# A fused patch-embedding, attention and mixture-of-experts kernel: an early piece of a table, stacked low-order products, block 0 gathered by matmuls

## The chip, the cores and the metric

The kernel runs on one core of one Trainium2 chip. The metric is the device time of one execution in microseconds (us); "before" is the median of three runs.

## What is computed

The reference joins three layers. Cut to what matters here (B = 8 batches, S = 164 tokens each, E = 192 columns, 12 heads, 16 experts):

```python
h = patches(x) @ proj_w.T + proj_b + pos_embed        # 36 image tokens a batch
h = concatenate([h, txt], axis=1)                     # + 128 text tokens = 164
# attention: xn = layernorm(layernorm(h)) * ln_w
avg_wte = mean(wte, axis=0)                           # wte is 50257 x 192
Q = xn[:, None] * W_qk[None, :, None, :]              # keys are the same as queries
attn = softmax(causal(Q @ Q.T / sqrt(192)))
out = (attn @ (xn - avg_wte)) / (position + 1)
h = h + out.reshape(B, S, 12 * 192) @ W_o.T
# switch layer: n = rmsnorm(layernorm(h)) * flnw, one expert of 16 a token,
# at most 64 tokens of a batch for one expert; the others get n itself
y = relu(n @ wi[e]) @ wo[e]
h = h + max_prob * where(kept, y, n)
```

## The kernel before

Everything stands in one program with a block of code for each engine; the order of the work is written out by hand, and the engines meet in semaphores.

**Attention.** Iteration b (0 to 6) finishes batch b and begins batch b+1; batch 7 (LAST) has its own tail. The 164 tokens are cut in 128 (part A) and 36 (part B). Each batch has five rounds of scores on TensorE (`score(b, r)`, r = 0 to 2 for A, 3 and 4 for B), for each a row maximum on VectorE (`row_max`), exponentials on ScalarE (`exps`), factors on VectorE (`row_factor`), and the scaling of P on GpSimd (`normalise`). P is transposed on TensorE (`p_transpose(b, q)`), q = 3 giving the first 128 keys of the B rows and q = 4 their last 36 keys. To multiply P and V exactly enough, each is split into a high and a low part (ScalarE copies the high part, `t_copy`, `values`; VectorE subtracts, `t_low`, `value_low`), and three products are added: high P by high V, high P by low V, low P by high V. `value(b, g)` does this into the banks bO (128 columns) and bE (the other 64 of a pair of heads); g = 3 is the round of the B rows, with 18 matmuls: three on the first 128 keys and three on the last 36, for each of one bO group and two bE groups. `project` multiplies by W_o into bank bJ.

**The table's mean.** The table has 28 chunks of 14 x 128 rows. Four chunks are loaded into four slots by SP; 18 more are added to them by accumulating DMAs that GpSimd issues (`add_wte`), each behind the one before it in the same slot; six are loaded in 12 half pieces by SP (`plain_loads`) into one buffer of two halves, and summed on VectorE (`plain_sum(b, k)`, two halves of columns for each of two half pieces). At the end VectorE adds the slots (`slot_add`) and reduces them (`table_total`, which ends with `wsum`); TensorE turns that into the mean (`wte_mean`), and `mean_projected` into a row that `mean_rows` subtracts from the token rows H. `h_transpose(n)` needs those rows.

**Switch layer.** After LAST's rows are finished, VectorE works out each token's expert and its place in a list of 112-row blocks (`routed`, `keep`, `place`; stage 0 has nine of the eleven slots of 128 rows, stage 1 the last two). GpSimd scatters the rows with 11 indirect DMAs to the DRAM tensor `dispatched`; SP waits until all are in (`scattered`), reads three blocks of rows back, and TensorE transposes the first (`x_transpose`). Each block then takes 12 matmuls into bO, 6 into bE, and an indirect DMA to the output. Rows that no expert keeps are worked out on VectorE and written by further indirect DMAs (`drow`, `dropI`). `stay_warm` is a run of matmuls whose result nobody reads.

## Time and profile before

| | |
|---|---|
| median of 3 runs | 367.31 us (365.68 to 370.08) |
| profiled execution, device time | 367.87 us |
| its span, first to last instruction | 366.0 us |
| busy: PE / VectorE / GpSimd / ScalarE | 334.5 / 228.0 / 167.7 / 126.2 us |
| mean granted TensorE clock | 0.967 of full speed |
| moved by DMA | 74.29 MB, mean 203 GB/s |

The profiled execution is 1.87 us longer than its span. Engines: PE is TensorE, DVE is VectorE, ACT is ScalarE, POOL is GpSimd, SP the engine that only issues DMAs; a q behind an engine's name is its instruction queue.

### The profile page before, as it was taken

To read this page: it belongs to the slowest core of one execution; us is meant where nothing else is said; L and a number is where in the kernel's file an instruction comes from. 1 tells how busy PE (TensorE), PEld (TensorE's weight loads), DVE (VectorE), ACT (ScalarE), POOL (GpSimd) and SP (SyncE) were. 2 spreads that over 40 slices of the span, in tenths; PEclk is the share of its full clock that TensorE was granted. 3 is DMA by queue.
4 is the path that set the end of the run, shared out by engine and by line. 5 is a ranking of instruction groups with operands and counts; after the bars stand their busy time and mean duration, and the time that the engine had idled before them with its cause. 6 is when DMAs were issued, how large, how long until landed. Compare 5 with 4: busy or idle time off the path is not lost.

```text
span 366.0 us, 6697 instructions
## 1 busy us (share of the span) xinstructions
PE 334.5 (91%) x2336; PEld 306.0 (84%) x2336; DVE 228.0 (62%) x557; ACT 126.2 (34%) x437; POOL 167.7 (46%) x180
## 2 busy tenths in 40 slices
PE   8499969899999999999998979999949999999992
PEld 3388859799899898997997969999815999999991
DVE  0669768789688787796888977657485222222221
ACT  2056543552545436534545024446610111111110
POOL 3173943755854846657548011250661134444321
PEclk9969989999999999999999978999998999999997
DMA  8899999289999995799997969400232699999940
GB/s 252 264 430 282 260 247 217 77 170 230 219 232 230 196 239 143 139 236 270 246 211 199 324 191 289 112 2 1 100 107 73 183 293 266 266 264 260 266 118 17
DMA packets 21096, 74.29 MB, mean 203 GB/s; under 512 B 3540, under 2 KB 9173, under 8 KB 20306
## 3 DMA queue, kind: packets, MB, share of 16 engines
q1 hardware_dynamic: 11362, 43.16, 38.5%
q0 software_dynamic: 6800, 27.82, 37.0%
q10 hardware_dynamic: 2912, 3.04, 3.0%
q8 instruction: 12, 0.20, 0.2%
q14 instruction: 10, 0.08, 0.1%
HBM read 66.12 MB, written 9.25 MB: 206 GB/s over the span
## 4 chain that ended last, share of the span: by engine, by line
PE 66%; DVE 13%; DMA 8%; ACT 5%; issue 5%; ACTq 1%; POOL 0%; POOLq 0%; DVEq 0%
PE bO L1224 18%; PE bS L1224 15%; PE bE L1224 14%; PE bJ L1224 12%; DMA wx<-in_wte 6%; ACT PB L563 2%; DMA hB<-in_txtB 2%; PE bT L1311 2%; DVE wx L856 1%; PE bT L1576 1%; DVE wbuf L856 1%; PE bT L1317 1%; PE bT L1270 1%; DVE oTA L823 1%; ACT pay L620 1%
## 5 line engine op out<-in xcount | busy, mean ns | idle before, releaser
L423 POOL TENSOR_TENSOR PA<-PA,rn 128x512 f32<-128x512 f32 x24 | 25.4, 1057 | 81.5 <-DVE rn L813 81.5
L401 POOL TENSOR_TENSOR AwA<-zT,w 96x512 f32<-96x512 f32 x45 | 50.1, 1192 | 17.4 <-ACT zT L540 17.4
L1224 PE MATMUL bJ<-wo_sb,oTA 128*128 128x192 f32 x288 | 52.7, 333 | 0.0
L558 ACT ACTIVATE PA<-bS,negmax 128x128 f32<-128x128 f32 x96 | 34.0, 367 | 51.3 <-DVE negmax L801 51.2
L1224 PEld LDWEIGHTS bS<-zT,AwA 96*128 96x128 f32 x384 | 47.3, 194 | 1.3 <-issue 0.2
L1224 PEld LDWEIGHTS bJ<-wo_sb,oTA 128*128 128x128 f32 x288 | 47.4, 194 | 0.0
L1224 PE MATMUL bS<-zT,AwA 96*128 96x128 f32 x384 | 47.1, 276 | 0.0
L1224 PE MATMUL bO<-PA,wx 96*128 96x112 f32 x384 | 45.4, 275 | 0.5 <-DVE PA L1197 0.5
L1224 PEld LDWEIGHTS bO<-PA,wx 96*128 96x128 f32 x384 | 44.9, 192 | 0.7 <-DVE PA L1197 0.7
L468 POOL DMA_INDIRECT out<-PA,yrow x16 | 15.1, 942 | 56.0 <-DVE PA L1213 56.0
L695 ACT ACTIVATE AwA<-bO 128x448 f32<-128x448 f32 x16 | 8.7, 544 | 78.5 <-PE bO L1224 52.9
L1224 PE MATMUL bE<-wx,AwA 128*112 128x192 f32 x192 | 33.9, 326 | 0.0
L838 DVE TENSOR_REDUCE wx<-wx 128x672 f32 (+1 forms) x24 | 31.7, 1326 | 2.2 <-DMA wx<-in_wte 2.2
L1224 PEld LDWEIGHTS bE<-wx,AwA 128*112 128x112 f32 x192 | 30.4, 177 | 0.0
L1206 DVE TENSOR_SCALAR AwA<-bO 128x224 f32<-128x224 f32 x16 | 6.3, 392 | 36.7 <-PE bO L1224 36.7
L576 ACT ACTIVATE oTA<-bO,lncol 128x512 f32<-128x512 f32 x24 | 16.6, 692 | 13.3 <-PE bO L1224 13.3
L801 DVE TENSOR_REDUCE negmax<-bS 128x4 f32<-128x512 f32 x24 | 16.4, 685 | 6.7 <-PE bS L1224 6.6
L1224 PE MATMUL bS<-zT,AwB 96*108 96x164 f32 x128 | 20.3, 302 | 0.0
L463 POOL DMA_INDIRECT dispatched<-pay,posI x11 | 12.4, 1125 | 16.3 <-ACT pay L620 12.1
L558 ACT ACTIVATION_READ_ACCUMULATOR PA<-bS,negmax 128x1 f32 x96 | 19.7, 205 | 0.0
L823 DVE TENSOR_SCALAR oTA<-bE,lncol 128x256 f32<-128x256 f32 x24 | 11.5, 480 | 12.8 <-PE bE L1224 12.8
L1224 PE MATMUL bO<-wo_sb,oTB 128*96 128x192 f32 x108 | 18.1, 327 | 1.0 <-DVE oTA L823 0.7
(252 smaller groups left out, 705.5 us busy)
## 6 DMA issues: line engine op xcount, KB each, us to landing
wbuf<-in_wte POOLq DMA_DIRECT2D x10, 1344.0 KB, 12.7
wx<-in_wte POOLq DMA_DIRECT2D x8, 1344.0 KB, 12.0
wx<-in_wi SPq DMA_DIRECT2D x16, 576.0 KB
wx<-in_wo SPq DMA_DIRECT2D x16, 576.0 KB
wx<-in_wte SPq DMA_DIRECT2D x12, 672.0 KB, 9.2
dispatched<-zeros SPq DMA_DIRECT2D x7, 675.5 KB, 9.0
wbuf<-in_wte SPq DMA_DIRECT2D x2, 1344.0 KB, 7.0
wx<-in_wte SPq DMA_DIRECT2D x2, 1344.0 KB, 17.6
```

Source lines behind the costliest of these rows:

```text
L401: nc.gpsimd.tensor_tensor(o, zT[:, k, ss].unsqueeze(1).to_broadcast(list(o.shape)), w2[:, k, hs].unsqueeze(2).to_broadcast(list(o.shape)), ...
L423: nc.gpsimd.tensor_tensor(t, t, q.unsqueeze(2).to_broadcast(list(t.shape)), ALU.mult).then_inc(p_ready, 1)
L463: nc.gpsimd.indirect_dma_start(out=xd[:, :], out_offset=bass.IndirectOffsetOnAxis(ap=posI[0:n, j:j + 1], axis=0), in_=pay[0:n, j, :], in_o ...
L468: nc.gpsimd.indirect_dma_start(out=out[:, :], out_offset=bass.IndirectOffsetOnAxis(ap=idx, axis=0), in_=rows, in_offset=None, bounds_check ...
L558: last = nc.scalar.activation(PA[:, h, :], bank[:, j * SA:(j + 1) * SA], ACT.Exp, bias=negmax[:, h:h + 1], accum_out=lsum[:, h:h + 1])
L563: last = nc.scalar.activation(PB[:, q, :], bank[0:HB * SB, j * SEQ:(j + 1) * SEQ], ACT.Exp, bias=negmax[0:HB * SB, 12 + q:13 + q], accum_o ...
L576: nc.scalar.activation(dst, src, ACT.Copy, scale=lncol[:, 0:1]).then_inc(o_used, 1)
L695: nc.scalar.activation(hT[:, 0:4, :], bO[0][:, 0:4 * T].rearrange("p (c n) -> p c n", c=4), ACT.Relu).then_inc(h0_ready, 1)
L801: nc.vector.tensor_reduce(negmax[:, 4 * r:4 * r + 4], bS[r % 2][:, :].rearrange("p (h s) -> p h s", h=4), X, ALU.max, negate=True).then_in ...
L823: nc.vector.tensor_scalar(dst, src, lncol[:, 1:2], None, ALU.mult).then_inc(e_used, 1)
L838: nc.vector.tensor_reduce(psums.rearrange("p (n e) -> p n e", e=EMB)[:, ds(2 * b + h, 1), q].rearrange("p n e -> p (n e)"), plain[h].rearr ...
L1224: return nc.tensor.matmul(o, l, r, start=start, stop=stop, skip_group_check=True)
```

## The change

Seven edits are made at once.

1. **Head.** The text rows are loaded in two parts, batches 0 and 1 first. The B rows (`hB`) are loaded three times, into partitions 0, 36 and 72. The w2 factors and the statistics of batches 0 and 1 come first on DVE; those of the other batches, the factors of batch 1 and the variances of batches 2 to 7 are moved.
2. **Plain piece.** SP issues the first plain piece ahead of the loads of slots 2 and 3; `plain_sum(0, 1)` stands behind `row_max(1, 1)`.
3. **Adds.** Iteration 0 issues one add instead of two, and iterations 1 to 5 three each (before 3, 3, 2, 3, 3).
4. **Stack.** The last 36 keys' high V, low V and high V lie in one tensor at partitions 0, 36 and 72 (the low one is written over), and P's in the same way, so that one matmul of 108 rows takes the place of three. GpSimd writes the last keys' P three times (`last_keys`). `value(b, 3)` has 12 matmuls.
5. **Table's sum.** In iteration 6, TensorE does `project(b, 0, 4)`, `p_transpose(b, 4)` and `score(LAST, 1)` ahead of `wte_mean`; on DVE `row_max(LAST, 0)` and `t_low(6, 3)` stand within `table_total`, and `mean_rows` stands behind `value_low(LAST)`.
6. **Block 0.** `select` writes for each slot a matrix of 112 columns that is one where a token's place is that column; TensorE multiplies the normalised rows by it (`dispatch`), and the result is block 0, transposed. Block 1's rows are the first that are read from DRAM.
7. **Dropped rows.** Their products are spread over the first two blocks, and the number of blocks is read behind block 0.

```diff
 # SP
             for s in range(2):
                 sp.dma_start(wchunk[s], wv[:, s, :]).then_inc(wte_first[s], 16)
             sp.dma_start(wo_sb[:, :, :], wo_attn).then_inc(wo_in, 16)
+            sp.wait_ge(tok_ready, 5)
+            plain_loads(sp, 0, 1)
             for s in range(2, WBUF):
                 sp.dma_start(wchunk[s], wv[:, s, :]).then_inc(wte_first[s], 16)
...
-            for q in range(XBUF - 1):
+            for q in (1, 0, 2):
                 rows(sp, q, q)
 # GpSimd
+            def last_keys():
+                for q0 in (0, 2):
+                    t, k = PB[:, q0:q0 + 2, SEQ:SEQ + SR].rearrange("p q (t s) -> p q t s", t=3), PB[:, q0:q0 + 2, SA:SEQ]
+                    nc.gpsimd.tensor_tensor(t, k.unsqueeze(2).to_broadcast(list(t.shape)),
+                                            rn[0:HB * SB, 12 + q0:14 + q0].unsqueeze(2).unsqueeze(3).to_broadcast(list(t.shape)),
+                                            ALU.mult).then_inc(pb_ready, 1)
...
                 weigh(b + 1, n, (0, 1), (1,))
                 for c in chunks[0:1]:
...
+                last_keys()
                 weigh(b + 1, n, (0, 1), (2,))
...
-                iteration(b, range(WBUF + 2 + 16 * b // 6, WBUF + 2 + 16 * (b + 1) // 6))
+                c = WBUF + 3 * b
+                iteration(b, range(c, c + 3) if b else (None, WBUF + 2))
 # DVE, head
+            dve.wait_ge(hb_in, 48)
+            text_stats(0, 2)
...
-            dve.wait_ge(vz_ready, 3)
+            dve.wait_ge(vz_ready, 2)
             z(0)
+            factors(1, 2, 2)
             dve.wait_ge(t_used, 1)
...
-            factors(1, 2, 2)
+            dve.wait_ge(hb2_in, 48)
+            text_stats(2, NBATCH)
             row_max(0, 0)
...
             row_factor(0, 2)
+            variances(2, NBATCH)
 # DVE, iteration(b)
-                plain_sum(b, 1)
+                else:
+                    plain_sum(b, 1)
                 t_low(b, 3)
                 row_factor(b + 1, 0)
                 t_low(b, 4)
                 row_max(b + 1, 1)
+                if is0(b):
+                    plain_sum(b, 1)
                 plain_sum(b, 2)
 # PE, value(b, 3)
                     else:
                         oo = o[:, 0:HEADS * SB].rearrange("p (h s) -> p h s", h=HEADS)
-                        mm(oo, vA[x][:, 0:E0], PTB0[y][:, :, :], i == 0, False)
-                        last = mm(oo, vB[x][:, 0:E0], PTB1[y][:, :, :], False, i == 2)
+                        last = mm(oo, vA[x][:, 0:E0], PTB0[y][:, :, :], i == 0, False)
+                if g == 3:
+                    last = mm(oo, vB[:, 0:E0], PTB1[:, :, :], False, True)
 # PE, iteration 6 and behind stage 1
                 p_transpose(b, 3)
-                if final:
-                    wte_mean()
                 project(b, 0, 4)
-                if final:
-                    mean_projected()
                 p_transpose(b, 4)
                 score(b + 1, 1)
                 if final:
-                    h_transpose(0)
+                    wte_mean()
                     pe.wait_ge(jb_used, 2)
                 value(b, 3)
                 if final:
-                    h_transpose(1)
+                    mean_projected()
                 project(b, 4, 10)
                 if final:
-                    h_transpose(2)
+                    h_transpose(0)
...
+            def dispatch(k0, k1):
+                for j in range(k0, k1):
+                    j0, _, sel = sels[j >= 6]
+                    for k in range(2):
+                        last = mm(bT[1][0:EC, k * T:(k + 1) * T], norm[:, j, k * EC:(k + 1) * EC], sel[:, j - j0, :],
+                                  j == 0 and k == 0, j == SLOTS - 1)
+                return last
...
+                if start:
+                    stay_warm(bJ, 6)
+                    x_transpose(1, 16)
 # DVE, behind place(B)
+            def select(B):
+                k0, k1 = STAGE[B]
+                link(nc.vector.tensor_tensor(part(posG, B), part(drop, B), part(posF, B), ALU.add))
+                for j0, j1, sel in sels:
+                    lo, hi = max(j0, k0), min(j1, k1)
+                    if lo < hi:
+                        bc = [128, hi - lo, T]
+                        nc.vector.tensor_tensor(sel[:, lo - j0:hi - j0, :], cst2[:, C_IO:C_IO + T].unsqueeze(1).to_broadcast(bc),
+                                                posG[:, lo:hi].unsqueeze(2).to_broadcast(bc), ALU.is_equal).then_inc(sel_ready, 1)
```

In iteration 6, DVE's order from the end of the table's sum (`wsum`) to the subtraction of the mean from the rows H (`H<-H,cN`), first before the change:

```order
L872 TENSOR_TENSOR wsum<-wsum,wtail 81x192
L877 TENSOR_TENSOR H<-bO,H 96x192
L801 TENSOR_REDUCE negmax<-bS 128x4
L958 SCALAR_TENSOR_TENSOR wr_sb<-bO,wr_sb 96x32
L962 TENSOR_SCALAR avg<-bO 128x2
L818 TENSOR_TENSOR PTB0L<-bT,PTB0H 128x432
L811 RECIPROCAL rinv<-lsum 128x4
L813 TENSOR_SCALAR rn<-rinv,cst 128x4
L966 TENSOR_SCALAR cN<-bO,cst 128x192
L967 COPY cS<-bO 128x192
L971 TENSOR_TENSOR H<-H,cN 128x768 x2
```

and with it, from `avg` on:

```order
L1004 TENSOR_SCALAR avg<-bO 128x2
L833 TENSOR_REDUCE negmax<-bS 128x4
L856 TENSOR_SCALAR oTB<-bE,lncol 128x6x36
L843 RECIPROCAL rinv<-lsum 128x4
L845 TENSOR_SCALAR rn<-rinv,cst 128x4
L861 TENSOR_TENSOR vAL<-zA,vAH 128x128
L863 TENSOR_TENSOR vAL<-zA,vAH 128x64
L861 TENSOR_TENSOR vB<-zB,vB 36x128
L863 TENSOR_TENSOR vB<-zB,vB 36x64
L1008 TENSOR_SCALAR cN<-bO,cst 128x192
L1009 COPY cS<-bO 128x192
L1013 TENSOR_TENSOR H<-H,cN 128x768 x2
```

The copy of value round 3 (`oTB`), a row factor and the four subtractions of `value_low` now stand between the mean and the rows from which it is subtracted.

PE's order in the same iteration, behind the last transposes of P's first 128 keys, before the change:

```order
L1315 MATMUL bT<-cst,PB 128x108 x4
L1224 MATMUL bO<-one,wsum 128x1
L1224 MATMUL bO<-one,wsum 64x1 x2
L1224 MATMUL bO<-wr_sb,one 96x16 x2
L1224 MATMUL bJ<-wo_sb,oTA 128x192 x4
L1224 MATMUL bO<-ws,avg 128x192 x2
L1317 MATMUL bT<-cst,PB 36x108 x4
```

and with it:

```order
L1386 MATMUL bT<-cst,PB 128x108 x4
L1293 MATMUL bJ<-wo_sb,oTA 128x192 x4
L1388 MATMUL bT<-cst,PB 108x108 x4
L1293 MATMUL bS<-maskA,idb 128x512
L1293 MATMUL bS<-zT,AwA 128x128 x8
L1293 MATMUL bO<-one,wsum 128x1
L1293 MATMUL bO<-one,wsum 64x1 x2
```

A projection, the last transposes and a round of scores moved ahead of the first matmul that needs `wsum`.

PE's order from the last ranks (`kp`) to block 0's first matmuls (`bO<-PA,wx`), before the change; 26 of the `bJ<-ones` rows are a run of `stay_warm`:

```order
L1224 MATMUL bT<-kp,ones 128x16
L1224 MATMUL bJ<-ones 128x512 x10
L1224 MATMUL bS<-cst,beC 1x27
L226 TENSOR_LOAD nbI
L226 ISA x2
L1224 MATMUL bJ<-ones 128x512 x26
L1576 MATMUL bT<-cst,AwA 96x112 x2
L1224 MATMUL bO<-PA,wx 128x112 x12
```

and with it:

```order
L1293 MATMUL bT<-kp,ones 128x16
L1293 MATMUL bT<-PA,pay 96x112 x6
L1293 MATMUL bT<-AwA,pay 96x112 x6
L1293 MATMUL bJ<-ones 128x512 x8
L1293 MATMUL bT<-AwA,pay 96x112 x4
L1293 MATMUL bS<-cst,beC 1x27
L1293 MATMUL bO<-PA,wx 128x112 x12
L1293 MATMUL bE<-wx,AwA 112x192 x6
L1293 MATMUL bJ<-ones 128x512 x6
L1662 MATMUL bT<-cst,AwA 96x112 x2
L234 TENSOR_LOAD nbI
```

Block 0 no longer stands behind the read of its rows (`bT<-cst,AwA`); that read is now block 1's.

## Rows read from the trace of the kernel before

**Rows 1.** The page: PE's granted clock in 40 equal slices of the span.

```profile
PEclk9969989999999999999999978999998999999997
```

**Rows 2.** Busy time by stretch: PE, PEld, DVE, ACT, POOL (instructions), PE's clock, DMA share, GB/s.

```profile
97.00:122.00 25.00, 24.45 (x177) 22.87 (x177) 19.86 (x37) 11.92 (x47) 16.03 (x17) 1.00 1.00 222
```

**Rows 3.** The chain of waits, in order of time: start us, us, what.

```profile
3.13 8.47 DMA hB<-in_txtB
...
27.30 20.47 DMA wx<-in_wte
...
78.71 1.18 PE bO L1224 x6
79.89 1.33 PE bE L1224 x12
...
103.55 1.17 PE bO L1224 x6
...
197.68 3.94 DVE wx L856 x2
...
226.97 1.95 PE bJ L1224 x12
229.36 2.00 PE bS L1224 x17
```

**Rows 4.** Instructions in order of time, the head: start us, us, what [idle before <- releaser].

```profile
14.81 0.35 DVE L750 TENSOR_TENSOR H<-bT,cS 36x192 f32<-36x192 f32 x1
...
18.96 0.45 PE L1270 MATMUL bT<-cst,zA 128*96 128x128 f32 x1 [4.81 <-DVE zB L795]
...
19.84 4.43 PE L1224 MATMUL bO<-wx 128*96 128x216 f32 x12
...
24.11 0.38 PE L1224 MATMUL bS<-maskA,idb 128*128 128x512 bf16 x1
```

**Rows 5.** The same view, iteration 0, DVE and PE.

```profile
43.01 2.63 DVE L773 TENSOR_SCALAR nmr<-mv 128x12 f32<-128x12 f32 x1
...
47.79 2.47 DVE L838 TENSOR_REDUCE wx<-wx 128x96 f32<-128x672 f32 x2 [1.56 <-DMA wx<-in_wte]
...
51.77 0.70 PE L1224 MATMUL bO<-PTB0H,vAH 128*128 128x432 f32 x1 [3.65 <-DVE PTB1L L818]
```

**Rows 6.** DMA queues between 36 and 42 us (q0: GpSimd's adds; q1: SP's).

```profile
q0 software_dynamic: 206, 1.02, 83.5%
q1 hardware_dynamic: 211, 0.43, 21.1%
```

**Rows 7.** Instructions in order of time: the last add, and SP's first zeros behind all adds.

```profile
184.30 1.20 POOL L412 DMA_DIRECT2D wbuf<-in_wte  x1
...
195.82 5.43 SPq L323 DMA_DIRECT2D dispatched<-zeros  x4
```

**Rows 8.** The same view, iteration 6.

```profile
214.86 0.69 PE L1224 MATMUL bO<-one,wsum 128*128 128x1 f32 x6 [2.67 <-DVE wsum L872]
...
221.08 1.83 DVE L971 TENSOR_TENSOR H<-H,cN 128x768 f32<-128x768 f32 x2
...
228.51 1.83 POOL L401 TENSOR_TENSOR AwB<-zT,w 96x432 f32<-96x432 f32 x2
```

**Rows 9.** The same view, from the last scatters to block 1.

```profile
272.58 2.54 DVE L1185 TENSOR_TENSOR H<-pay,flnb 128x1152 f32<-128x1152 f32 x4
273.56 2.37 POOL L463 DMA_INDIRECT dispatched<-pay,posI  x1 [0.30 <-issue]
...
277.60 1.27 SPq L242 DMA_DIRECT2D AwA<-dispatched  x3
280.68 0.36 PE L1576 MATMUL bT<-cst,AwA 112*96 112x112 f32 x2
...
281.51 2.93 PE L1224 MATMUL bO<-PA,wx 96*128 96x112 f32 x24 [0.48 <-DVE PA L1197]
...
286.43 2.83 PE L1224 MATMUL bO<-PA,wx 96*128 96x112 f32 x24
```

252 lines of the change are left out of this document (150 added, 102 removed).

## The prediction

> **What bounds the kernel now.** I read the granted clock by slices first, then the busy time by stretch, then the chain of waits, and last the single instructions wherever the chain leaves PE. PE's clock is full nearly everywhere, but lower in the slices from 18 us (a 6), from 46 us (an 8) and from 210 us (a 7 and an 8) [rows 1]; there the engine ran for some us at 1.2 instead of 2.4 GHz. In the body PE is the bound: 24.45 of 25 us busy at full clock [rows 2], and one batch follows the other in 103.55 - 78.71 = 24.84 us [rows 3]. The chain leaves PE in four places: at the head (the load of the B rows, 8.47 us, then the statistics), in iteration 0 (a plain piece that takes 20.47 us to land), at the table's sum in iteration 6, and at the scatter before block 0 [rows 3, 9]. Each low clock stands behind an idle time of PE there: 4.81 us, 3.65 us and 2.67 us [rows 4, 5, 8]. So an idle time costs itself and the slow matmuls after it. The change touches all four places and takes matmuls from the body. I name times of the trace of before throughout, as if nothing had shifted.
>
> **Head.** DVE begins the image rows at 14.81 [rows 4], because it first waits until 11.6 (3.13 + 8.47, [rows 3]) for all B rows and then works out eight batches of statistics. With a small first load it can begin when TensorE's image products and the first text rows are there. No row shows that moment apart; it lies between 10.8 and 12.5 by the order of the loads, and I take 11.2. From there to PE's transposes of z it is 18.96 - 14.81 = 4.15 us, less some 0.6 for the w2 steps that now come first: 14.8. PE is then hardly idle (its embedding ended at 18.96 - 4.81 = 14.15), so its clock should stay up, and the 4.43 us of the second embedding become 2.2 [rows 4]. The first scores, at 24.11, then begin at about 14.8 + 5.15 - 2.2 = 17.8: 6.3 us. Against it stand 432 KB more for the threefold B rows, for which SP's table loads wait: I put these 1 to 3 us later, so that GpSimd stands at its second add and scales the first P late. PE has gaps there that take most of that. Term: **-5.8** (bounds -4.0 and -6.5).
>
> **Iteration 0.** PE waits 3.65 us for the low parts before value round 3, since DVE stood 1.56 us for the plain piece and then summed two quarters of it, 2.47 us [rows 5]. The piece was behind slots 2 and 3 (2.75 MB) in SP's queue and beside GpSimd's adds. It now stands ahead of these slots. Beside the adds SP's queue moves 0.43 MB in 6 us (0.072 MB/us, [rows 6]), at worst 9.6 us for half a piece of 0.69 MB: issued at about 27 it lands before 38, while DVE wants it at 46. The Trainium skill, DMA: Bandwidth & Descriptors, "Queues, rings and completion order", says that each DMA engine goes round robin between the queues, a packet each. By that, SP's queue would get about half (0.12 MB/us of the same 0.24) and half a piece would take 5.7 us; the row's two queues moved 1.02 and 0.43 MB, so the trace does not bear out an equal share. Both end in time.
> What is late next is DVE itself. The 2.63 us of `nmr`, during which GpSimd weighed without pause [rows 5], goes from this place to where DVE is about to begin `t_low(0, 0)`; it may meet the scaling of P there and costs about 1.3 us before PE's first value round. One quarter sum, 1.24 us, is left ahead of `t_low(0, 3)`. I get value round 3 ready as PE ends `score(1, 1)`, so 3.65 us of idle time fall away and 1.3 are given back. Term: **-2.4** (bounds -0.5 and -3.7).
> From this round to the next one PE needs 78.47 - 51.77 = 26.7 us now (78.47 being where the round that the chain lists from 78.71 begins), against 24.84 in the body: slow clock and DVE's late rows [rows 3, 5]. With the idle time gone I expect the body's pace. The stack's saving belongs to it. So 26.7 - 24.0 = 2.7, less 0.4 because the add of iteration 0 must wait for slot 2, which now loads behind the piece: **-2.3** (bounds -0.5 and -2.9).
>
> **Stack.** Value round 3 takes 1.18 us for six matmuls into bO and 1.33 for twelve into bE [rows 3]. Two of six and four of twelve go: 0.39 + 0.44 = 0.84 us of PE. GpSimd pays for it: two more instructions of 216 columns; two of 432 took 1.83 us [rows 8], so 0.9 us, less 0.3 since the scaling has fewer columns. It ends about 1.2 us before PE's last transposes, and GpSimd is busy 16 of 25 us [rows 2]: nothing on the path; without that cover it would cost 0.6 us a batch. But PE and DVE are both nearly late here: DVE waited only some 0.65 us for that round, so its rows come at most 0.65 earlier. I take 0.68 a batch, for batches 1 to 5: **-3.4** (bounds -2.0 and -4.2). Batch 6 is in the next term. In LAST it gives nothing: behind it PE waits for a copy that DVE does after `place(0)`.
>
> **Adds.** Three a batch instead of 2.7. At 83.5% of 6 us for 1.02 MB [rows 6] an add of 1.376 MB costs 6.8 us of all engines, and at 21.1% for 0.43 MB a piece costs 4.1. Three adds and a piece: 24.4 us in a batch of 24.0 to 24.2, so the queue grows by 0.2 to 0.4 us a batch, 2 in all. The last add was issued at 184.30 and all had landed at 195.82; DVE needs it at 197.68 + 3.94 = 201.6 [rows 3, 7]. 5.8 us of cover less 2: **0**; beyond the cover each us costs a us.
>
> **Table's sum.** DVE's chain from 197.68 to `wsum` is unbroken; row maximum and `t_low` within it put its end at 216.3 instead of 214.8. PE fills the time with a projection (1.3 us; twelve records took 1.95), transposes (0.5) and scores (2.0, [rows 3]), and the 2.67 us of idle time and the slow clock behind it go [rows 8]. Value round 3 ends at 219.5 and the projection of six at 222.1. But then PE wants the mean subtracted. `mean_rows` now stands behind `value_low(LAST)`, which needs the exponentials of `score(LAST, 1)` and ScalarE's copies (222), and whose two-input subtractions wait behind GpSimd's AwB pair, 1.83 us [rows 8]: done at 224.2. Then 0.8 for the two copies and 0.9 for the first half of 1.83 us: 226.0. PE stands 3.9 us, more than the idle time it was spared, and comes back at half clock, which cost 2 to 3 us before. From there to the end of the projections I count 6.4 us at full clock plus 2.2: 234.7 against about 234.2 now, with the stack's 0.84 in it. Term: **+0.4** (bounds -2.0 and +2.0).
>
> **Block 0.** Before, SP reads the rows at 277.60, they are transposed at 280.68, block 0 begins at 281.51 and block 1 at 286.43 [rows 9]. Now block 0 needs only the places. These are known at 271.5; `select` has 224 columns in stage 1, and DVE's 2112 columns took 2.54 us [rows 9], so 0.3; the last four products (112 columns each, 24 records took 2.93 us) 0.9, the copy 0.4: block 0 begins near 273.6, 8 us early. Stage 0's `select`, 1.4 us, lies in DVE's wait for `project_b(2)`, and its 18 products take the place of `stay_warm`. But block 1 still needs the scatter: rows at 277.6, transposed at 280.7, started at 281.5, against 286.43. So only one block's time is won, 4.9, and a little more since the last scatter, 2.37 us beside DVE's products against about 1.0 for the others, now runs before them. I take 0.4 of it. Term: **-5.3** (bounds -3.5 and -6.2). The Trainium skill, SBUF — State Buffer, "Who interferes with whom", says that of a DVE instruction with two SBUF inputs and a GpSimd instruction that reads SBUF the second is fully blocked until the first ends. By that the 1.4 us would all go and the read come at 276.2, though PE is ready only at 280.0, so 5.6; the same rule is against the moved `nmr` and `value_low`, and the rows' 2.63 us agrees. The dropped rows' products lie in DVE's waits of the first two blocks: 0.
>
> **Sum.** -5.8 - 2.4 - 2.3 - 3.4 + 0.4 - 5.3 = -18.8. From the profiled 367.87 us: 349.1. The median of before lies 0.56 lower: **348.5 us**.
>
> **Rivals.** (1) The table's part goes well: DVE isn't held up in `value_low`, PE's idle time stays short and the clock up. For it: PE also went on at full clock behind small gaps. Against it: four instructions ahead of `mean_rows`. It gives 3 more: 345.5; 20%. (2) The adds land late: the body shortens by 0.7 a batch while the DMA engines were full already (share 1.00, [rows 2]). From 5.8 us of growth on, DVE waits at `slot_add`; at 10 it gives 353; 12%. (3) Block 0 does not give what it says: the added DVE and PE work delays the scatter, or block 1's rows land a block's time later: 353.8; 8%. (4) Slower than before: an accumulating add takes 8.3 us or more instead of 6.8 when three a batch stand beside the pieces. Then 15 adds need over 23 us more than DVE's cover and every gain is gone; at 9 us, 15 x 2.2 - 3.8 = 29 us of waiting give 378. Against it: 4.13 MB of adds went through in the 25 us of [rows 2], whose window holds three; 2%. The forecast has 55%; 3% I leave for more than (1).
>
> **How the numbers follow.** The range reaches over (1) and most of (2) and (3) and holds the bounds of head and table, which are the widest: 342.5 to 354.5. A measurement of this kernel can tell about 1% (3.7 us) from no change. Faster by more than that: all but (4) and a sliver, 97%; within 1%: 1%; slower: 2%.
>
> **What the profile after would show.** Right: the first scores near 18 us, PE's clock full until 40 us, no wait of DVE for the plain piece, 24.1 us a batch, an idle time of PE before the first rows of H are transposed, block 0's first matmul 8 us before block 1's rows are transposed. Wrong: half clock in the first 25 us, DVE waiting for an add at `slot_add`, or a second slow stretch behind iteration 0. The forecast fails most easily by the table's term and by the head, whose start no row shows.

## The result, and the profile after

The changed kernel takes 355.26 us, the median of 4 runs (351.50, 355.12, 355.41 and 355.53), against 367.15 us before (4 runs, 365.68 to 370.08). The ratio is 0.9643, with a 95% interval of 0.9555 to 0.9731. So the kernel is faster, as forecast, but by 11.9 us instead of 18.8, and the median lies 0.8 us above the end of the range. (The forecast was built on 367.31 us; 0.9643 of that is 354.2, just inside.) The profiled execution took 355.53 us (span 353.7) against 367.87. Executions that ran over 1.5% longer than the fastest of their kernel (four, two of them with the plain piece back and one of the last version) are left out where I compare.

First three lines of the page of the kernel after: the clock granted to PE, the DMA engines' share and their rate, in 40 slices of the span.

```profile
PEclk9998999999999999999999998999999999999997
DMA  7799999499999999999997979300338799999940
GB/s 242 157 420 274 297 350 251 74 244 244 194 240 249 207 226 224 246 233 286 214 207 234 283 206 273 89 2 1 114 118 240 230 285 237 231 222 247 239 117 11
```

The low clocks of [rows 1] from 18 and from 46 us are gone. One 8 stands from 27 us, where PE now waits for the scaling of P(0), and one from 212 us, behind the table's sum. (The 8 that [rows 1] has from 274 us, which the prediction doesn't list, fell on warming products, whose results nobody reads.) In the last quarter the DMA engines are full (six slices of 9), and in the last five of these they move 222 to 247 GB/s, against 260 to 266 in the kernel before. That line turns out to be the important one.

The chain of waits after, in order of time, answers to [rows 3]:

```profile
5.22 10.43 DMA hB<-in_txtB
16.11 9.69 DMA wbuf<-in_wte
26.10 1.23 POOL wbuf L422
...
46.60 2.58 DVE wx L871 x2
50.21 3.55 DVE vB L861
...
324.02 17.33 DMA wx<-in_wi
341.48 2.90 PE bO L1293 x24
```

At 26.10 GpSimd's second add is on it, at 50.21 DVE's low parts, neither of them before. The last two are new as well: the weights of the last block landed 17.33 us after their issue, and PE stood for them. To see where the time went, I followed the start of value round 3 of every batch (`vA[0]` against `PTB0`, 432 columns) and `xt_copy` of every block, since both stand in both kernels.

| us from the span's start | before | after | gained in all | forecast |
| --- | --- | --- | --- | --- |
| first scores (mask) | 24.11 | 17.93 | 6.2 | 6.3 |
| value round 3, batch 0 | 51.77 | 45.59 | 6.2 | 8.2 |
| value round 3, batch 1 | 78.47 | 71.19 | 7.3 | 10.5 |
| value round 3, batch 5 | 177.64 | 167.71 | 9.9 | 13.2 |
| value round 3, batch 7 | 252.76 | 241.88 | 10.9 | 13.5 |
| block 1, first matmul | 286.43 | 269.88 | 16.6 | 18.8 |
| last `xt_copy` | 356.99 | 344.73 | 12.3 | 18.8 |

(The forecast column adds up the prediction's terms in their order.) Two stretches missed: 3.2 us up to batch 1, nearly all of it behind the first scores, and 4.3 us in the blocks, where the forecast had nothing. The rest came out 1.0 us better.

**The head.** Instructions of the kernel after in order of time, to be held against [rows 4]:

```profile
11.39 0.35 DVE L778 TENSOR_TENSOR H<-bT,cS 36x192 f32<-36x192 f32 x1
...
15.06 0.31 PE L1339 MATMUL bT<-cst,zA 128*96 128x128 f32 x1 [1.45 <-DVE zB L827]
...
15.54 2.35 PE L1293 MATMUL bO<-wx 128*96 128x216 f32 x12
17.93 0.38 PE L1293 MATMUL bS<-maskA,idb 128*128 128x512 bf16 x1
...
26.10 1.23 POOL L422 DMA_DIRECT2D wbuf<-in_wte  x1 [2.90 <-DMA wbuf<-in_wte]
26.89 2.50 POOL L433 TENSOR_TENSOR PA<-PA,rn 128x512 f32<-128x512 f32 x2
...
26.40 3.15 DVE L861 TENSOR_TENSOR vAL<-zA,vAH 128x128 fp32r<-128x128 f32 x1
...
28.46 0.69 PE L1382 MATMUL bT<-cst,PA 128*128 128x128 f32 x4 [3.37 <-POOL PA L433]
```

DVE's image rows stand at 11.39 (estimated 11.2), z's transposes at 15.06 (14.8), the embedding takes 2.35 us (2.2) at full clock. Behind that two things are seen that the sum lacked. GpSimd waits 2.90 us for slot 1 before it can issue its second add, the scaling of P(0) stands behind it, and PE waits 3.37 us. And DVE's subtraction for the low parts, of two tiles in SBUF, takes 3.15 us where 0.28 is usual: it ends as GpSimd's run of work (26.10 to 29.39) ends.

**Block 0 to block 1**, PE of the kernel after, against [rows 9]:

```profile
262.98 2.93 PE L1293 MATMUL bO<-PA,wx 96*128 96x112 f32 x24 [0.34 <-DVE PA L1231]
...
269.05 0.36 PE L1662 MATMUL bT<-cst,AwA 112*96 112x112 f32 x2
269.88 2.93 PE L1293 MATMUL bO<-PA,wx 96*128 96x112 f32 x24 [0.48 <-DVE PA L1231]
```

Between batch 7's value round 3 and block 1, 28.0 us are left of 33.7: 5.7 us gained. Block 0's first matmul stands 6.1 us before block 1's rows are transposed. The prediction said 8, though its own times (273.6 and 280.7) give 7.1.

**The blocks.** Busy time by stretch in two stretches of 20 us that begin 18 to 20 us behind the start of block 1, before and after (PE, PEld, DVE, ACT, POOL, PE's clock, DMA share, GB/s). Before:

```profile
304.00:324.00 20.00, 20.00 (x159) 20.00 (x158) 5.07 (x18) 2.18 (x4) 8.32 (x9) 1.00 1.03 271
324.00:344.00 20.00, 20.00 (x158) 20.00 (x157) 4.94 (x16) 2.18 (x4) 7.57 (x8) 1.00 1.03 258
```

After:

```profile
289.00:309.00 20.00, 19.94 (x156) 19.58 (x155) 4.78 (x15) 2.17 (x4) 7.59 (x8) 1.00 1.03 241
309.00:329.00 20.00, 19.87 (x153) 19.19 (x151) 4.73 (x16) 2.17 (x4) 7.64 (x9) 1.00 1.03 233
```

The share is the same 1.03, so the engines are full in both; what they move fell from 258 to 271 GB/s to 233 to 241. Before, all 14 blocks behind block 1 took 4.81 us each. After, they do so until 297 us; the rest lose 4.2 us in all, 1.4, 1.5 and 0.5 of it on the last three.

The trace also shows how such a loss builds up. There are four places for weights, so a block's weights are asked for when the fourth block before it ends. In the change the `wi` load, half of a block's weights, took about 5 us from issue to landing for the first blocks served in this way and then ever longer, up to 17.3 us for the last. In the run with GpSimd's changed order (below), whose blocks lost nothing, it ended at 12.7 us, and there 14.1 us lie between this issue and the start of the block (323.2 and 337.3). So the blocks live on a stock of loaded weights that shrinks even at full engines, and the large losses come when it is used up. The trace of before doesn't hold these landings.

### The profile page after: what moved, and what is told of

Read it like the earlier page. It is cut to its first block, busy times and chain, and to the rows that moved or that the text cites. A ratio compares the mean times of both kernels' runs of the same rounds, so it can differ in the third digit from the quotient of the medians.

```text
span 353.7 us, 6667 instructions
## 1 busy us (share of the span) xinstructions
PE 322.4 (91%) x2304; PEld 298.4 (84%) x2304; DVE 225.1 (64%) x562; ACT 125.9 (36%) x437; POOL 171.3 (48%) x194
## 4 chain that ended last, share of the span: by engine, by line
PE 60%; DVE 14%; DMA 14%; ACT 5%; issue 4%; ACTq 1%; POOL 1%; POOLq 0%; SPq 0%; DVEq 0%
PE bS L1293 18%; PE bO L1293 13%; PE bJ L1293 11%; PE bE L1293 11%; DMA wx<-in_wi 5%; DMA hB<-in_txtB 3%; DMA AwA<-dispatched 3%; ACT PB L588 3%; DMA wbuf<-in_wte 3%; PE bT L1382 2%; DVE wx L889 1%; DVE vB L861 1%; DVE oTA L856 1%; DVE wbuf L889 1%; ACT PA L583 1%
## 5 line engine op out<-in xcount | busy, mean ns | idle before, releaser
L411 POOL TENSOR_TENSOR AwA<-zT,w 96x512 f32<-96x512 f32 x45 | 49.6, 1170 | 17.0 <-ACT zT L565 17.0
L1293 PE MATMUL bJ<-wo_sb,oTA 128*128 128x192 f32 x288 | 51.7, 328 | 0.0
L1293 PEld LDWEIGHTS bJ<-wo_sb,oTA 128*128 128x128 f32 x288 | 46.6, 191 | 0.0
L1293 PE MATMUL bS<-zT,AwB 96*108 96x164 f32 x128 | 21.4, 313 | 0.0
L601 ACT ACTIVATE oTA<-bO,lncol 128x512 f32<-128x512 f32 x24 | 16.6, 693 | 13.2 <-PE bO L1293 13.2
L1293 PEld LDWEIGHTS bS<-zT,AwB 96*108 96x108 f32 x128 | 19.5, 181 | 0.1
L1276 DVE CAST yrow<-AwA 112x1 int32<-112x1 f32 x16 | 2.4, 148 | 27.0 <-DMA out<-PA,yrow 27.0
```

The lines of the kernel that those rows point to most:

```text
L411: nc.gpsimd.tensor_tensor(o, zT[:, k, ss].unsqueeze(1).to_broadcast(list(o.shape)), w2[:, k, hs].unsqueeze(2).to_broadcast(list(o.shape)), ...
L601: nc.scalar.activation(dst, src, ACT.Copy, scale=lncol[:, 0:1]).then_inc(o_used, 1)
L1293: return nc.tensor.matmul(o, l, r, start=start, stop=stop, skip_group_check=True)
```

## The experiments

All are the changed kernel with the edit shown. They ran in three groups of four, each on one chip with its own runs of the kernel before (medians 367.80, 368.18 and 367.58 us). Only the first group holds the change itself, so the later ones are compared with it across chips. I call the time that the blocks behind block 1 take beyond 4.81 us each **the blocks' loss**, in the profiled execution.

**The change again, unaltered.**

> The changed kernel unaltered, as the measure for the other three and to see whether its profile repeats. In the first profile the blocks run at 4.81 us each up to 297 us and then lose 4.2 us to rows and weights that land late (three of them, 1.4 + 1.5 + 0.5 us, behind 320 us), while the DMA engines move 237 GB/s against 269 before. Theory A: this is what the chip's memory gave in that execution; then this profile may show none of it and about 351.5 us, as one of the four runs did. Theory B: it belongs to the changed kernel; then the blocks lose 3 to 5 us again and the time is 355 to 356.

354.71 us (354.23 to 355.98); ratio 0.9641 (0.9595 to 0.9688). The blocks' loss is 4.2 us again, at 246 and 253 GB/s in the same two stretches. Theory B, as far as two profiles can say. In front of the blocks the repeat isn't the same: value round 3 comes at 46.16 in batch 0, 72.70 in batch 1 and 242.34 in batch 7.

**Block 0 started as before.**

```diff
-            select(0)
-            select(1)
-            dispatch(...)                  # all 22 products
+            stay_warm(bJ, 26)
+            x_transpose(0, 16)
...
-            for q in (1, 0, 2):
+            for q in (0, 1, 2):
```

> The changed kernel with block 0 started as before: no select, no products that pick its rows, its rows loaded behind the scatter and transposed, the dropped rows computed ahead of the blocks. Theory A (the late loss is of the memory, not of this part): the blocks start 5 to 6 us later (block 1 at about 275.5 instead of 269.9) and the whole is 5 to 6 us slower than the changed kernel, if both have or both lack the late loss. Theory B (the early start causes the late loss): the blocks keep 4.81 us to the end, and the whole is only 1 to 2 us slower than the changed kernel, about 357.

The products of the dropped rows go back ahead of the blocks as well. 361.78 us (360.67 to 362.83), 7.1 above the unaltered change. PE in order of time:

```profile
268.47 0.40 PE L1649 MATMUL bT<-cst,AwA 112*96 112x112 f32 x2 [2.25 <-DMA AwA<-dispatched]
269.35 5.12 PE L1286 MATMUL bO<-PA,wx 96*128 96x112 f32 x24 [0.48 <-DVE PA L1229]
...
277.55 2.83 PE L1286 MATMUL bO<-PA,wx 96*128 96x112 f32 x24
```

From batch 7's value round 3 (240.84) to block 1's first matmul are 36.7 us against 28.0 in the change and 33.7 before. 3.1 of the 8.7 are not the part's worth: the warming products end 2.25 us before the rows are there, and block 0's first matmuls then run at 1.2 GHz (5.12 us against 2.93, and 3.08 against 2.17 for the second set; granted clock 0.56 from 269 to 275 us). The rest is 5.6, theory A's size. The blocks' loss is still 1.8 us with the old start. So the loss is not made by block 0's early start alone; theory B falls, the more so as six runs below keep the early start and lose nothing.

**GpSimd scales before its second add.**

```diff
             add_wte(WBUF)
+            normalise(0, (0,))
             add_wte(WBUF + 1)
-            normalise(0, range(3))
+            normalise(0, (1, 2))
```

> The changed kernel with one edit at the head: GpSimd scales the first quarter of P(0) before it issues the second add, which now waits 2.9 us for its slot. Theory: that wait holds PE 3.4 us before the first transposes of P (28.46 to 31.10), and with it gone PE is 2 to 3.4 us earlier at value(0,3); the whole is 2 to 3 us shorter. Rival: DVE's rows of PT or the second add, issued later, become the bound at once, and the time moves by less than 1 us.

351.77 us (350.22 to 353.57), 2.9 below the unaltered change, just what the theory said, and yet it is not the reason. PE's wait for P falls only from 3.4 to 2.2 us, value round 3 of batch 0 stands at 45.17, and DVE copies block 1's transposed rows at 269.40, 0.04 earlier than in the first profile and 0.52 earlier than in the second. The profile's gain lies in the blocks: their loss is 0.0, at 253 and 252 GB/s. The median alone would have confirmed a wrong theory. The rival is right on the head: other waits come at once. Value round 3 of batch 1 stands at 72.18, 1.0 later than in the change. One of these waits is DVE's, in iteration 0:

```profile
50.15 3.97 DVE L765 TENSOR_TENSOR nwz<-rstd 128x12 f32<-128x12 f32 x1
```

12 columns take 3.97 us (0.17 in the change), while GpSimd issues an add, scales and weighs from 50.04 to 54.08 us without a gap. PE then waits 1.86 us for ScalarE, and its clock is at half from 60 to 62 us.

**SP does not wait for the rest of the B rows.**

```diff
-            sp.wait_ge(hb2_in, 48)
```

> The changed kernel, but SP no longer waits for the second part of the B rows (batches 2 to 7) before it loads the table's slots. Theory: the slots are then loaded 2 to 3 us earlier (about 13.3 instead of 15.7 us), the second add is issued by 24 us, and the scaling of P no longer waits: 1.5 to 3 us shorter at value(0,3) and at the end. Rival: the slots' transfers, now beside the B rows and the row sums' inputs, hold up the statistics of batches 2 to 7, and the gain is under 1 us.

357.15 us (356.51 to 358.77), 2.4 *above* the unaltered change: both expectations fell. The slots do come earlier, but ScalarE's small loads, which it issues behind `pat2_in`, now stand beside them. The chain:

```profile
14.09 22.18 DMA flc<-in_flnw
```

ScalarE's first copy of PT waits for them, PE waits 8.3 us, and value round 3 of batch 0 comes at 50.74 instead of 45.6 to 46.2. The wait for the B rows is a pace for the small loads, too.

**The dropped rows' transfers beside the last four blocks.**

```diff
-                if 2 <= b < 2 + SLOTS:
-                    drops(b - 2)
+                if b >= EXP - 4:
+                    for j in range(3 * (b - EXP + 4), min(SLOTS, 3 * (b - EXP + 5))):
+                        drops(j)
```

> The changed kernel with one edit in the blocks: GpSimd sends the 11 dropped-row transfers beside the last four blocks (three a block), when no weights are loaded any more, instead of one beside each of blocks 2 to 12. Theory A: the blocks lose their 4.2 us because the DMA engines are full and these rows (11 x 98 KB, 1.08 MB, about 4.5 us at 240 GB/s) come on top of the weights; then blocks 2 to 15 keep 4.81 us, the loss is under 1 us, and the time is 3 to 4 us below the changed kernel (354.7 and 355.3 us): about 351. Theory B: the DMA engines move less in these executions for a reason of their own, whatever is queued (239 to 254 GB/s in the profiles so far against 267 before); then 1 to 3 us of loss stay and the time is above 353. Rival C, slower: the rows sent last end behind the last block and add up to 2 us.

356.57 us (355.33 to 356.93); ratio 0.9679 (0.9650 to 0.9708). The blocks' loss is 0.0, and the engines move 274 and 280 GB/s, the most of all profiles. Most of what is won there is paid at the end, by a rival that I had priced at 2 us. GpSimd's last two issues:

```profile
347.43 0.99 POOL L490 DMA_INDIRECT out<-H,dropI  x1 [0.30 <-issue]
348.72 0.92 POOL L490 DMA_INDIRECT out<-H,dropI  x1 [0.30 <-issue]
```

An issue takes GpSimd 1.2 to 1.3 us with its gap, four a block are 5.0 us against a block of 4.81, and the last rows of y queue behind them: from the last `xt_copy` to the end of the span it is 12.3 us instead of 9.0. So 3.3 us of the 4.2 won are paid back. The remaining 1.7 us of this profile lie ahead of block 1, in PE's clock (next run).

**The table's sum back at its old place.** PE's and DVE's steps around `wte_mean`, `mean_projected`, `h_transpose` and `mean_rows`, and ScalarE's `nt_copy`, in the order of before.

> The changed kernel with the table's sum and the mean put back where they were (PE: ahead of the first projection, the four transposes of H between the later steps as before; DVE and ScalarE in their old order), all else of the change kept. Theory: the reorder moved an idle time from one place to another; PE again waits about 2.7 us behind its scores and runs slowly behind it, instead of 3.3 us before the first transposes, and the time is within 1 us of the changed kernel (354.7 to 355.3). Rival: the reorder spares the slow clock, and without it the kernel is 2 to 3 us slower, about 358.

352.15 us (351.11 to 354.58); ratio 0.9556 (0.9532 to 0.9581), below the change's. In the profile the time from value round 3 of batch 5 to that of batch 7 is 74.4 us. With the new order it is 74.2 and 73.2 in the two profiles of the change and 72.9 to 75.5 in the others, two of which show why it varies. Busy time of the same stretch, and the first transposes of H, in the run with GpSimd's changed order and in that with the late dropped rows:

```profile
207.00:225.00 18.00, 15.28 (x101) 14.77 (x102) 13.49 (x34) 7.35 (x27) 5.01 (x5) 0.91 0.95 263
216.92 0.64 PE L1511 MATMUL bO<-cst,H 128*96 128x128 f32 x4 [2.28 <-DVE H L1014]
```

```profile
207.00:225.00 18.00, 14.42 (x83) 13.81 (x82) 12.42 (x31) 5.88 (x24) 4.57 (x5) 0.81 0.95 263
217.04 0.64 PE L1511 MATMUL bO<-cst,H 128*96 128x128 f32 x4 [3.14 <-DVE H L1014]
```

The kernels have the same instructions here, and PE idles twice: 0.8 to 0.9 us for `wsum`, then 2 to 3 us for H. In the first of these runs the clock fell behind the short idle time alone (0.50 from 210 to 212 us, 1.00 from 217 to 221): 73.2 us. In the second it fell behind both (0.50 from 208 to 210 and from 218 to 220): 75.5 us. In the change's own profile it fell behind the second alone: 74.2 us. So the same stretch varies by 2.3 us with where the clock falls. The place of the table's sum is worth less than this, in either direction. That this run's median is lower isn't explained by the table, as far as its profile tells, which is of the slowest of its four executions (354.58 us): block 1 stands where it stood (its rows at 269.65 against 269.44 and 269.92), and the blocks lost 2.6 us instead of 4.2.

**The row maximum ahead of the low parts, in iteration 0.**

```diff
+                if is0(b):
+                    row_max(b + 1, 2)
                 value_low(b + 1)
```

> The changed kernel, with DVE in iteration 0 taking the third row maximum of batch 1 before the low parts of the values instead of behind them. In the profile one of those subtractions takes 3.63 us (0.28 elsewhere), as long as GpSimd works without a gap beside it, the maximum comes 3.3 us late, and PE then waits 1.4 us for ScalarE's exponentials. Theory: both engines' two-input work from SBUF shuts the other out; the subtraction is held as long again, but the maximum, which reads PSUM alone, is out of its way, the 1.4 us fall away, and value round 3 of batch 1 comes 1.4 us earlier. Rival: DVE only waits for the scores there and the rows of z come later in turn; then PE waits elsewhere and less than 0.5 us is won.

353.72 us (351.41 to 354.62). Value round 3 of batch 1 stands at 71.20, against 71.19 in the change: nothing won. The rival is right. DVE finds the scores ready only at 51.83, and the low parts (2.04 us) and z shift behind GpSimd in turn. The blocks' loss is 0.0 here, at 265 and 269 GB/s, and batches 5 to 7 took 75.4 us.

**Three edits together**: the two orders (with two quarters of P(0) scaled before the second add) and the late dropped rows.

> The changed kernel with three edits: the dropped rows sent beside the last four blocks; the third row maximum of batch 1 before the low parts of the values; and GpSimd scaling the first two quarters of P(0) before it issues the second add (one quarter before it gave 0.5 us at the first block, the rest of that kernel's 3 us lay in the blocks). If the gains add up: 3 to 4 us in the blocks, 1.4 in iteration 1 and 1 to 1.5 at the head, about 349 us, against 354.7 to 355.3 of the changed kernel. Rival: the adds of the table become the bound of iteration 6, since they are issued as late as before and the body is earlier; then DVE waits at the slots' sum and 1 to 2 us of it are lost.

354.11 us (353.02 to 355.05). Block 1 is 2.5 us earlier than in the first profile of the change (its rows at 266.90), the blocks lose 0.5 us (265 and 257 GB/s), but 5 us go again behind the last block (13.8 us instead of 9.0). So the gains in front add up in part, and the late rows take them.

**The plain piece back behind slots 2 and 3.**

```diff
-            sp.wait_ge(tok_ready, 5)
-            plain_loads(sp, 0, 1)
             for s in range(2, WBUF):
...
-            plain_loads(sp, 1, WPLAIN)
+            sp.wait_ge(tok_ready, 5)
+            plain_loads(sp, 0, WPLAIN)
```

> The changed kernel with the first plain piece back behind slots 2 and 3 and the small loads in SP's queue, all else kept. Theory: the piece lands behind 50 us, DVE waits for it again between the row maximum and the low parts of PT, PE has an idle time of 3 to 5 us before value round 3 of iteration 0 (45.6 to 46.2 us so far) and a slow clock behind it; that round comes at 48.5 us or later and the whole is 2 to 4 us slower, while the add of iteration 0 no longer waits for slot 2 (1.6 us of GpSimd). Rival: the shorter wait of GpSimd repays it, and the first block moves by less than 1 us.

359.75 and 363.35 us in the two executions compared (all four: 359.75 to 367.94), 4 to 9 us above the change's 354.7 to 355.3. Instructions in order of time, from the one of 363.35:

```profile
52.32 1.28 DVE L870 TENSOR_REDUCE wx<-wx 128x96 f32<-128x672 f32 x1 [8.61 <-DMA wx<-in_wte]
...
55.26 0.70 PE L1292 MATMUL bO<-PTB0H,vAH 128*128 128x432 f32 x1 [8.20 <-DVE PTB L850]
```

The theory's place is right, its size is not. Value round 3 of batch 0 comes at 55.26, 9.7 us later than in the change and 3.5 later than before it, and block 1 12.0 us later than in the change. (At the end it is 7.8, as these blocks lost nothing, at 272 and 258 GB/s.) The first half of the piece lands at 52.30 us, before the change at 47.76, since the slots ahead of it are themselves loaded later. DVE's wait, 1.56 us in [rows 5], is 8.61, and PE's clock is at half from 52 to 60 us. So this part decides whether the head's gain arrives.

**The saving of the stack undone on PE.**

```diff
-                    last = mm(oo, vB[:, 0:E0], PTB1[:, :, :], False, True)
+                    for n in range(3):
+                        last = mm(oo, vB[:, 0:E0], PTB1[:, :, :], False, n == 2)
```

> The changed kernel with TensorE's saving of the stack undone: each of the three stacked matmuls of a value round 3 is issued three times (six matmuls more a batch). The last 36 keys' products are so added three times, and the outputs are other numbers; layout, copies and GpSimd's work stay as changed. Theory: value round 3 takes 0.84 us more, PE is the bound of the body, and the period of 24.11 us grows by 0.7 to 0.85 us; over batches 1 to 5 that is 3.5 to 4.2 us, and batches 0, 6 and 7 add up to 1.5: 359 to 360 against 354.7 to 355.3. Rival: what is saved in the body comes from GpSimd's or DVE's part of the stack, and the period stays at 24.1 to 24.3.

The three matmuls into bE are issued three times in the same way. 364.42 us (363.12 to 365.27). PE in order of time:

```profile
96.89 0.44 PE L1293 MATMUL bO<-PTB0H,vAH 128*128 128x432 f32 x1
...
97.55 0.75 PE L1293 MATMUL bO<-PTB,vB 128*128 128x432 f32 x3
...
121.74 0.44 PE L1293 MATMUL bO<-PTB0H,vAH 128*128 128x432 f32 x1
```

The period is 24.85 us, that of before (24.84), against the change's:

```profile
95.38 0.44 PE L1293 MATMUL bO<-PTB0H,vAH 128*128 128x432 f32 x1
...
119.49 0.44 PE L1293 MATMUL bO<-PTB0H,vAH 128*128 128x432 f32 x1
```

24.11 us. So the whole of the body's gain is PE's fewer matmuls. Of the 9 us in the median, 4.8 are something else: with other numbers the tokens went otherwise, and there are 17 blocks instead of 16. They lost nothing, at 269 and 266 GB/s.

**The two orders alone.**

> The changed kernel with two of the three edits of the run before: the maximum ahead of the low parts in iteration 0, and GpSimd scaling two quarters of P(0) before its second add; the dropped rows beside blocks 2 to 12 as in the change. Theory: block 1 begins at 266.9 us as there (269.9 in the change), the tail behind the last block is 9 us again instead of 13.9, and the blocks lose 0 to 4 us by what the DMA engines move (none at 250 GB/s and more, 4 at 240): a span of 347.5 to 351.5, a median of 350 to 352. Rival: DVE's wait for the table's last adds shows in iteration 6 and takes 1 us.

351.74 us (351.06 to 351.87); ratio 0.9542 (0.9478 to 0.9605). The blocks' loss is 0.0, at 256 and 251 GB/s. But block 1's rows are at 269.05, not at 266.9. Value round 3 of batch 0 comes 3.4 us earlier than in the change (42.24), that of batch 1 only 0.3 (70.86). (With the same two orders it was 1.2 in the run with three edits and is 1.4 in the next one, where PE's clock stayed up.) The rows between them, GpSimd and DVE:

```profile
50.51 1.23 POOL L422 DMA_DIRECT2D wx<-in_wte  x1 [5.88 <-DMA wx<-in_wte]
51.31 1.51 POOL L433 TENSOR_TENSOR PA<-PA,rn 128x512 f32<-128x512 f32 x1
52.31 2.23 POOL L411 TENSOR_TENSOR AwB<-zT,w 96x432 f32<-96x432 f32 x2
...
50.66 4.01 DVE L828 TENSOR_SCALAR zB<-hB,rstd,nmr 108x192 f32<-108x192 f32 x1
```

The chain of waits leads from there to SP's load behind the piece:

```profile
21.64 28.59 DMA wx<-in_wte
```

GpSimd stands 5.88 us in the add of iteration 0, since slot 2 is loaded behind the plain piece and lands at 50.2. The scaling of P(1) and the last weights for its scores stand behind the add. In the change the same wait is 1.60 us, ending at 49.58: behind an early plain piece the add isn't issued before 49.6 us, whatever goes before it. Most of the head's further gains end there.

**The two orders, and the dropped rows beside blocks 10 to 14.**

```diff
-                if 2 <= b < 2 + SLOTS:
-                    drops(b - 2)
+                first = {10: 0, 11: 2, 12: 4, 13: 6, 14: 9}.get(b, SLOTS)
+                for j in range(first, {10: 2, 11: 4, 12: 6, 13: 9, 14: SLOTS}.get(b, 0)):
+                    drops(j)
```

> The same two orders, and the dropped rows sent beside blocks 10 to 14, two a block (three at block 13), so that GpSimd, which needs 1.24 us for each issue, is through with them before the last block. Theory: half of the 1.08 MB then falls to a time in which no weights are loaded, the blocks lose under 1 us, the tail stays 9 us, and the median is 348 to 350, below the version with the dropped rows beside blocks 2 to 12 by 1 to 2 us. Rival: blocks 10 and 11 still load weights, whose last ones come late with twice the dropped rows beside them, and nothing is won over the other version.

355.04 us (354.39 to 356.46; the execution left out took 362.74), 3.3 us above the version with the rows beside blocks 2 to 12; the rival is right. No block loses anything but the last, which loses 5.3 us (252 and 245 GB/s), here in the chain of waits:

```profile
322.18 15.57 DMA wx<-in_wi
337.88 2.90 PE bO L1298 x24
```

Its weights are the last that are loaded, and the dropped rows now crowd just them.

## Why the prediction was right, and where it was not

**The head** (-5.8; measured -6.2 at the first scores) was right in mechanism and size for what leads up to these scores. What failed is the sentence on what stands against it, "PE has gaps there that take most of that", by which 6.3 became 5.8. SP's table loads went out 3.3 us later (15.71 instead of 12.44), past my 1 to 3, GpSimd stood 2.90 us in its second add, and PE 3.37 us behind it. PE's clock was then at half from 30 to 32 us, where the prediction had it full until 40. The shorter wait in the run with the changed GpSimd order (2.2 us) gained 0.4 us at value round 3, and two quarters ahead of the add gained 3.4. So the cause is shown; it was a wait in GpSimd's queue that I had named and priced at 0.5 us.

**Iteration 0** (-2.4 and -2.3; measured 0.0 and -1.1, and in the repeat -0.3 and -0.2). The plain piece did what it should: DVE no longer waits for it, and PE's 3.65 us are gone. They were taken back by the 3.37 us above. That the piece's place is needed was understated: put back, value round 3 comes 9.7 us later. From batch 0 to batch 1 I expected the body's pace and 0.4 us for the add that waits for slot 2. 25.6 us were measured against 24.4 forecast. The step that failed is this 0.4. The add waits for slot 2 until 49.6 to 50.6 us in both profiles of the change and with every order of GpSimd that was tried, and in the change DVE stands 3.63 us beside what GpSimd does behind it; PE then waits 1.4 us for ScalarE. It is DVE's stand that costs, not the add's wait itself: in the run with block 0's old start, whose code is the same up to there, the same subtraction took 1.20 us beside the same work of GpSimd, PE waited 0.3 us, and the stretch took 24.5 us, as forecast. In the repeat PE's clock fell behind the wait of 1.4 us and the stretch took 26.5 us.

**The stack** (-3.4) was right: 0.68 a batch forecast, 0.74 by undoing it (24.85 - 24.11 over one period), and 0.66 on average from batch 1 to batch 5 of the two profiles.

**The adds** (0) were right: DVE never waited at `slot_add`, in no run. Rivals (2) and (4) did not come.

**The table's sum** (+0.4): from batch 5 to batch 7 the change is 0.95 us shorter than before, and 0.7 of it is the stack's share for batch 5, which stands in its own term. So the term is -0.3, within its bounds, and -1.3 in the repeat. The forecast idle time was 3.9 us; it is 3.32, at `h_transpose(0)`, and the scores behind it take 3.02 us instead of 2.00:

```profile
215.34 0.64 PE L1510 MATMUL bO<-cst,H 128*96 128x128 f32 x4 [3.32 <-DVE H L1013]
...
216.03 3.02 PE L1293 MATMUL bS<-zT,AwA 96*128 96x128 f32 x16
```

Rival (1), by which this part goes well, needed a short idle time and a clock that stays up, and had neither. The price isn't a constant either: PE's clock fell at one of two places or at both, and these two batches took 72.9 to 75.5 us by that. In the repeat it fell earlier, behind the 0.84 us for `wsum`, and the wait for H was 2.29 us.

**Block 0** (-5.3) was right: 5.7 at block 1, and 5.6 by undoing it. 5.3 and the 5.6 by the lock rule of the Trainium skill (SBUF — State Buffer, "Who interferes with whom") lie too close together for these runs to part them.

**The blocks**: this is the larger miss, 4.2 us, and no term of the sum held it. I had ended the sum at block 1 and taken for granted that 4.81 us a block would last: the step that failed is this term of nothing, which measured 4.2. The page's DMA line of before has 9 there, and full engines leave only the stock of four weight places if their rate falls. Whether blocks lose goes with what the engines move in the two stretches of 20 us. Seven profiles with 251 GB/s or more in both lost nothing (before, GpSimd's order, late rows, row maximum, plain piece back, three products, two orders). Four with less in one of them lost: the two of the change 4.2 us (241 and 233; 246 and 253), the old start 1.8 (248 and 253), the old table 2.6 (248 and 247). The last run, 5.3 lost at 252 and 245, fits. Two speak against so plain a rule: without SP's wait the blocks lost 1.7 us at 256 and 251, and with three edits 0.5 at 265 and 257. With the dropped rows taken out of these stretches 274 and 280 were moved and nothing was lost, but the rows then harmed what came behind. **What sets the rate stays open.** Neither block 0's start (1.8 us lost with the old one) nor the order at the head (0, 1.7 and 4.2 us lost with the same block code) decides it, and the change's own runs, three at 355.1 to 355.5 and one at 351.5, fit a loss that comes and goes. Rival (3) came near in time (353.8) but by another mechanism: block 0 gave what it should.

Three of these kernels took about 3 us less than the change: the two orders 351.74 us, ratio 0.9542 (0.9478 to 0.9605), GpSimd's order 351.77 and the old table 352.15. For the first two most of that lies in the blocks' loss, not in the orders. The change itself ran once in 351.50. The obvious next step, the add of iteration 0 behind the last weights instead of ahead of the scaling, wasn't tried.

That the time lies at the edge of the range, and not further off, is in part luck. The range was wide because it reached over rivals that did not come, and the two misses are of no rival's kind.

## What to carry to other kernels

A stage that runs at full pace beside full DMA engines has to have a term in the sum, with the rate as its unknown: an earlier start of its matmuls doesn't help a stage once its transfers bound it. Look there at how the time from issue to landing grows from one load to the next, since a stock of buffers hides a slow rate until it is used up. When a median confirms a theory, look for the gain at its place in the profile; one of these runs gave the 2.9 us that was forecast, and 0.5 at most were there. And when a wait is taken away at the head, look in the queue of every engine for the next wait with a fixed time (here a load that lands at 50 us), since most gains before it end there.

## What the runs showed of the hardware

**PE's clock after the same idle time is not the same in every execution.** The two profiles of the change have PE idle 1.42 and 1.40 us ahead of the last round of batch 1's scores, with the same instructions on both sides. From 60 to 62 us the granted clock was 1.00 in the one and 0.50 in the other, and batch 0 to batch 1 took 25.6 and 26.5 us.

**A DVE instruction can last as long as a whole run of GpSimd's.** In the first two places where GpSimd issued an add and worked on behind it without a gap, the DVE instruction beside it took 3.15 and 3.63 us in the change, and 2.0 to 4.0 us in nearly all the other runs that keep these places, instead of 0.17 to 0.38. It ended within 0.2 us of GpSimd's run. In the change:

```profile
49.58 1.22 POOL L422 DMA_DIRECT2D wx<-in_wte  x1 [1.60 <-DMA wx<-in_wte]
50.37 1.50 POOL L433 TENSOR_TENSOR PA<-PA,rn 128x512 f32<-128x512 f32 x1
51.37 2.23 POOL L411 TENSOR_TENSOR AwB<-zT,w 96x432 f32<-96x432 f32 x2
```

```profile
50.12 3.63 DVE L861 TENSOR_TENSOR vB<-zB,vB 36x128 fp32r<-36x128 f32 x1
```

GpSimd's last instruction ends at 53.60, DVE's at 53.75. In the body it is otherwise. Beside the same scaling and weighing, DVE gets in between two of GpSimd's instructions:

```profile
98.51 1.03 POOL L433 TENSOR_TENSOR PA<-PA,rn 128x512 f32<-128x512 f32 x1 [1.86 <-DVE rn L845]
99.50 1.82 POOL L411 TENSOR_TENSOR AwB<-zT,w 96x432 f32<-96x432 f32 x2
```

```profile
99.61 0.93 DVE L863 TENSOR_TENSOR vAL<-zA,vAH 128x64 fp32r<-128x64 f32 x1
```

The Trainium skill, SBUF — State Buffer, "Who interferes with whom", has a DVE instruction with two SBUF inputs wait for the whole of a GpSimd instruction that came first. The body's 0.93 us agrees. The 3.15 to 4.01 us are more than any one of GpSimd's instructions there, so in these places it waited for the whole run. The add's issue ahead of the run doesn't explain it alone: with block 0's old start, where the issue stands at 50.01 us, DVE's instructions beside the same run took 1.20, 0.92 and 0.79 us. What decides stays open. In the run with the row maximum ahead, DVE's subtraction began at 52.44, 0.9 us after the issue had ended, and was still held for both weighings, to 54.48. Nor were they two-input instructions alone: `zB<-hB,rstd,nmr`, a TENSOR_SCALAR of one tile and two columns of scalars, took 4.01 us. The prediction's own row is of this kind: `nmr<-mv`, 2.63 us, is a TENSOR_SCALAR with one SBUF input, so the rule for two inputs, with which the prediction says it agrees, doesn't cover it. It ended at 45.64, GpSimd's two weighings at 45.60.
